# Splitting the second half's gated recurrence by time: eight steps ahead of the Runge-Kutta loop, twenty-four on GpSimd beside it

## The reference, cut to what matters

```
# x3: output of attention and MLP (B=32, T=32, D=256)
k    = x3 @ Wz.T + bz;   n = x3 @ Wn.T + bn
z    = sigmoid(k);       g(n) = n + 0.5 where n >= 0, else sigmoid(n)
h[t] = (1 - z[t]) * h[t-1] + z[t] * g(n[t]),   h[-1] = 0.5
x    = x + h                              # the "drive" of the ODE
q = p = cond
for t in range(32):                       # RK4, four derivative stages a step
    dq = q - q**3/3 - p + x[:, t] + tanh(q) @ coupling.T + bias
    dp = 0.08 * (q + 0.7 - 0.8 * p)
    q, p = rk4_step(...), clipped to +-20;   trace[:, t] = q
out = x + top4_blocks(gelu(trace @ W1.T)) @ W2.T
```

## Time and profile before

| | |
|---|---|
| median of three runs | 482.5 us |
| the profiled execution | 482.44 us |
| its span, first to last instruction | 480.6 us |
| TensorE busy | 467.4 us, 97% |
| VectorE busy | 389.3 us, 81% |
| ScalarE busy | 318.9 us, 66% |
| GpSimd busy | 48.0 us, 10% |

### The profile page before, as it was taken

One profiled execution on the slowest core, in us unless ns is written; L12 is line 12 of the kernel. 1 busy time (PEld: TensorE's weight loads), 2 busy tenths in 40 slices (PEclk: granted clock), 3 DMA queues, 4 the chain that ended last, 5 costly groups with the idle time before them and its releaser, 6 DMA issues.

```text
span 480.6 us, 13808 instructions
## 1 busy us (share of the span) xinstructions
PE 467.4 (97%) x5271; PEld 334.8 (70%) x5271; DVE 389.3 (81%) x1368; ACT 318.9 (66%) x950; POOL 48.0 (10%) x78
## 2 busy tenths in 40 slices
PE   7999999999999999999899999999999999999997
PEld 4455776557656676568545444788898988989886
DVE  4969895779768899997896997888888888888884
ACT  1677964788477966887476965565665656656563
POOL 3010240223020320223000000000000000000000
PEclk9999999999999999999999999999999999999999
DMA  8992510100201000000000000000000000000000
GB/s 283 419 388 70 135 45 22 62 25 23 66 22 44 22 0 2 0 2 1 1 1 1 0 1 0 3 3 1 0 1 11 12 0 12 0 12 11 1 12 23
DMA packets 10399, 20.85 MB, mean 43 GB/s; under 512 B 1472, under 2 KB 4992, under 8 KB 9728
## 3 DMA queue, kind: packets, MB, share of 16 engines
q1 hardware_dynamic: 9808, 19.89, 12.0%
q10 hardware_dynamic: 560, 0.60, 0.4%
HBM read 19.40 MB, written 1.08 MB: 43 GB/s over the span
## 4 chain that ended last, share of the span: by engine, by line
PE 88%; DVE 4%; ACT 3%; DMA 1%; issue 1%; POOL 1%; SPq 0%; DVEq 0%
PE bank L884 58%; PE score L884 27%; PE spare L884 2%; DMA ao_sb<-xtok 1%; POOL ptx L507 1%; ACT ptx L632 1%; ACT ao_sb L585 1%; DVE drive L1459 1%; ACT x L532 0%; ACT th L810 0%; DVE drive L1463 0%; DVE q_group L2112 0%; DVE tok_stats L1406 0%; DVE acc L1551 0%; DVE drive L1614 0%
## 5 line engine op out<-in xcount | busy, mean ns | idle before, releaser
L884 PE MATMUL bank<-x,pairs_store 128*128 128x512 f16 x384 | 86.3, 379 | 0.5 <-ACT x L532 0.4
L884 PEld LDWEIGHTS bank<-x,pairs_store 128*128 128x128 f16 x384 | 36.9, 98 | 43.4 <-issue 1.4
L507 POOL TENSOR_TENSOR ptx<-pt,ptx 32x256 f16<-32x256 f32 x62 | 43.2, 697 | 176.2 <-ACT ptx L632 172.8
L884 PE MATMUL score<-cub,neg_eye 128*128 128x64 f32 x256 | 55.6, 299 | 0.0
L585 ACT ACTIVATE big<-bank,head_b 128x512 f16<-128x512 f32 x60 | 39.8, 685 | 17.4 <-PE bank L884 17.0
L2026 DVE TENSOR_TENSOR thlo<-th 128x64 f16<-128x64 f32 x128 | 28.8, 225 | 26.0 <-ACT th L811 24.8
L884 PE MATMUL score<-th,coup_part 128*128 128x32 f16 x1024 | 46.2, 177 | 0.9
L884 PE MATMUL bank<-pairs_store,ao_sb 128*128 128x256 f16 x360 | 43.0, 273 | 0.7 <-issue 0.2
L884 PE MATMUL bank<-pairs_store,x 128*128 128x512 f16 x192 | 43.4, 379 | 0.0
L810 ACT ACTIVATE th<-score 128x64 f16<-128x64 f32 x96 | 21.5, 224 | 31.7 <-PE score L884 28.9
L884 PEld LDWEIGHTS bank<-pairs_store,ao_sb 128*128 128x128 f16 x360 | 34.0, 98 | 7.5 <-DVE ao_sb L1652 1.5
(11 more groups left out here) (252 smaller groups left out, 1052.1 us busy)
## 6 DMA issues: line engine op xcount, KB each, us to landing
wqk_sb<-wqk SPq DMA_DIRECT2D x16, 256.0 KB, 2.7
wv_sb<-wv SPq DMA_DIRECT2D x4, 512.0 KB, 5.4
wo_sb<-wo SPq DMA_DIRECT2D x4, 512.0 KB, 4.2
f_sb<-ffn_w SPq DMA_DIRECT2D x2, 1024.0 KB, 14.7
ao_sb<-xtok SPq DMA_DIRECT2D x4, 256.0 KB, 5.8
x_sb<-xT SPq DMA_DIRECT2D x1, 1024.0 KB, 12.5
w_sb<-w1T SPq DMA_DIRECT2D x1, 1024.0 KB, 16.1
w_sb<-w2T SPq DMA_DIRECT2D x1, 1024.0 KB, 16.9
```

Source lines behind the costliest of these rows:

```text
L507: nc.gpsimd.tensor_tensor(ptx[s, 1, :, s], pt[s], ptx[s, 0, :, s], ALU.subtract).then_inc(ptx_ready, 1)
L884: return nc.tensor.matmul(dst, lhsT, rhs, start=start, stop=stop, **kw)
```

## The change

The second half's columns are split by time instead of by batch. EARLY is steps 0 to 7 (16 batches x 8 = 128 columns a block, NE), LATE is steps 8 to 31 (384 columns a block, NL). TensorE multiplies EARLY of both blocks first. ScalarE makes three passes for a piece, all from PSUM: Tanh of z, Tanh of n, and Relu of n (the identity g = min(tanh, 0) + 1 + 2 relu, up to scale, replaces the first Relu). VectorE does EARLY of both blocks (`early_gru`), whose scan's last column is handed on.

LATE goes to GpSimd (`late_terms`): three tensor_scalar and two tensor_tensor passes of 384 columns, and the handed-on state folded into step 8 by two passes of 16 columns. VectorE scans LATE in eight pieces of 96 columns, at slot 1 of stages 6 to 13 of the loop's first round, in place of the eight low parts. GpSimd then adds x and splits the drive (`late_pair`): four passes of 384 columns a block, two of them written by time. A wait for both blocks' splits stands on VectorE at the second round's stage 15.

On ScalarE, `late_gates(0)` lies ahead of the EARLY drive's high parts, and `late_gates(1)`, three passes of 384 columns, after the first state's tanh, ahead of the loop. On TensorE the three matmuls that summed block 1's terms go, and 18 unread matmuls become 4.

```diff
-        za_last = centred[:, 0]
-        unit_row = pn[:].rearrange("p g t -> p (g t)").bitcast(F16)
+        EARLY, LATE = slice(0, 2 * UNROLL), slice(2 * UNROLL, T)
+        NBH = B // NH
+        NE, NL = NBH * 2 * UNROLL, NBH * (T - 2 * UNROLL)
+        parts_at = 2 * MB * P
+        early_store = big[:, parts_at:parts_at + KB * 6 * NE].rearrange("p (k w n) -> p k w n", k=KB, w=6)
+        parts_at += KB * 6 * NE
+        late_store = big[:, parts_at:parts_at + KB * 4 * NL].rearrange("p (k w n) -> p k w n", k=KB, w=4)
+        carry = sc[:, 0:KB, 0:NBH]
+        half_bn = tok_tmp[:, 0:KB]
...
-            nc.gpsimd.memset(unit_row, 1.0 / CSCALE).then_inc(unit_ready, 1)
+            def steps_of(ob):
+                return late_store[:, ob].rearrange("p w (b t) -> p w b t", b=NBH)
+            def later_steps(ap, ob):
+                return ap[:, ob, HALF:N].rearrange("p (b t) -> p b t", t=T)[:, :, LATE]
+            def late_terms(ob):
+                z, cand, pos, keep = (late_store[:, ob, w] for w in range(4))
+                use = USE_GRU[1] + ob
+                pool.wait_ge(free[bank_of(use)], count_of(use) + 1)
+                own.step(nc.gpsimd.tensor_scalar(keep, z, -0.5, 0.5, ALU.mult, ALU.add))
+                own.wait()
+                own.step(nc.gpsimd.tensor_scalar(z, z, 1.0, 0.25, ALU.add, ALU.mult))
+                pool.wait_ge(late_tanh, ob + 1)
+                own.step(nc.gpsimd.tensor_scalar(cand, cand, 0.0, 1.0, ALU.min, ALU.add))
+                use = USE_GRU[1] + 3 - ob
+                pool.wait_ge(free[bank_of(use)], count_of(use) + 1)
+                own.wait()
+                own.step(nc.gpsimd.tensor_tensor(cand, cand, pos, ALU.add))
+                own.wait()
+                own.step(nc.gpsimd.tensor_tensor(cand, cand, z, ALU.mult))
+                pool.wait_ge(z_used, KB + ob + 1)
+                _, cand, _, keep = (steps_of(ob)[:, w, :, 0] for w in range(4))
+                state = early_store[:, ob, 5].rearrange("p (b t) -> p b t", b=NBH)[:, :, 2 * UNROLL - 1]
+                own.step(nc.gpsimd.tensor_tensor(carry[:, ob], keep, state, ALU.mult))
+                own.wait()
+                own.step(nc.gpsimd.tensor_tensor(cand, cand, carry[:, ob], ALU.add))
+                own.wait()
+                nc.gpsimd.memset(keep, 0.0).then_inc(late_ready, 1)
+            def late_pair(ob):
+                at = slice(ob * B + NBH, (ob + 1) * B)
+                high, low = (drive_pair[:, c, LATE, at].rearrange("p t b -> p b t") for c in range(2))
+                shifted_drive = steps_of(ob)[:, 0]
+                pool.wait_ge(late_scanned, 4 * (ob + 1))
+                own.step(nc.gpsimd.tensor_tensor(later_steps(drive, ob), steps_of(ob)[:, 2], later_steps(x_sb, ob), ALU.add))
+                own.wait()
+                own.step(nc.gpsimd.tensor_scalar(shifted_drive, later_steps(drive, ob), c2_shifted[:, ob:ob + 1], None, ALU.add))
+                own.step(nc.gpsimd.tensor_scalar(high, later_steps(drive, ob), c2_shifted[:, ob:ob + 1], None, ALU.add))
+                own.wait()
+                nc.gpsimd.tensor_tensor(low, shifted_drive, high, ALU.subtract).then_inc(late_split, 1)
+            for ob in range(KB):
+                late_terms(ob)
+            for ob in range(KB):
+                late_pair(ob)
...
-            use = USE_GRU[1]
...
-            drive_bias(2, 4)
+            def gate_values(ob, z_in, n_in, out, z_done, tanh_done, n_done):
+                nc.scalar.activation(out[:, 0], z_in, ACT.Tanh, bias=hb[:, ob:ob + 1], scale=0.5).then_inc(z_done, 1)
+                if n_done is not early_gate:
+                    wait_product(USE_GRU[1] + 3 - ob)
+                nc.scalar.activation(out[:, 1], n_in, ACT.Tanh, bias=half_bn[:, ob:ob + 1], scale=0.5).then_inc(tanh_done, 1)
+                nc.scalar.activation(out[:, 2], n_in, ACT.Relu, bias=bn_twice[:, ob:ob + 1], scale=2.0).then_inc(n_done, 1)
+            def early_gates(ob):
+                src = (spare, score[:, 0])[ob]
+                act.wait_ge(early_full, ob + 1)
+                gate_values(ob, src[:, NE:2 * NE], src[:, 0:NE], early_store[:, ob], early_gate, early_gate, early_gate)
+            def late_gates(ob, both=True):
+                z_use, n_use = USE_GRU[1] + ob, USE_GRU[1] + 3 - ob
+                wait_product(z_use)
+                gate_values(ob, bank[bank_of(z_use)][:, 0:NL], bank[bank_of(n_use)][:, 0:NL], late_store[:, ob],
+                            free[bank_of(z_use)], late_tanh, free[bank_of(n_use)])
+            early_gates(0)
+            early_gates(1)
+            late_gates(0)
+            drive_bias(2, 3, EARLY)
+            drive_bias(3, 4, EARLY)
...
-            drive_bias(3, 5, slice(0, UNROLL))
-            drive_bias(3, 5, slice(UNROLL, T))
+            late_gates(1)
...
+                x3_steps = x3.rearrange("p k (b t) -> p k b t", t=T)
+                early_dst = (spare, score[:, 0])
+                def early(ob, k):
+                    for w, weights in enumerate((wn_sb, wz_sb)):
+                        last = mm(early_dst[ob][:, w * NE:(w + 1) * NE], weights[:, k, ob * P:(ob + 1) * P],
+                                  x3_steps[:, k, NBH:B, EARLY], k == 0 and w == 0, k == KB - 1, skip_group_check=True)
+                    return last
+                def late(use, weights, ob, k):
+                    dst = fill(use) if k == 0 else bank[bank_of(use)]
+                    last = mm(dst[:, 0:NL], weights[:, k, ob * P:(ob + 1) * P], x3_steps[:, k, NBH:B, LATE], k == 0, k == KB - 1)
+                    if k == KB - 1:
+                        last.then_inc(full[bank_of(use)], 1)
+                use = USE_GRU[1]
                 pe.wait_ge(x3_ready, KB + 1)
+                for ob in range(KB):
+                    early(ob, 0)
+                late(use, wz_sb, 0, 0)
                 pe.wait_ge(x3_ready, 2 * KB)
+                for ob in range(KB):
+                    early(ob, 1).then_inc(early_full, 1)
+                late(use, wz_sb, 0, 1)
+                for k in range(KB):
+                    late(use + 3, wn_sb, 0, k)
+                pe.wait_ge(early_gate, 3 * KB)
+                unread(score[:, 0], 1)
+                mm(score[:, 1], scaled_eye[:], ptx[:, 0, 0:G // 2].rearrange("p g n -> p (g n)"), True, True).then_inc(seeded, 1)
+                for k in range(KB):
+                    late(use + 1, wz_sb, 1, k)
+                for k in range(KB):
+                    late(use + 2, wn_sb, 1, k)
...
-            use = USE_GRU[1] + 2
...
-            unread(bank[bank_of(USE_GRU[1] + 1)][:], 18)
+            for use in (USE_GRU[1], USE_GRU[1] + 3):
+                pe.wait_ge(free[bank_of(use)], count_of(use) + 1)
+            unread(bank[bank_of(USE_GRU[1])][:], 4)
...
+            def early_gru(ob):
+                z, cand, pos, quarter, keep, state = (early_store[:, ob, w] for w in range(6))
+                dve.wait_ge(early_gate, 3 * ob + 1)
+                own.step(V.tensor_scalar(quarter, z, 1.0, 0.25, ALU.add, ALU.mult))
+                own.step(V.tensor_scalar(keep, z, -0.5, 0.5, ALU.mult, ALU.add))
+                dve.wait_ge(early_gate, 3 * ob + 3)
+                own.step(V.scalar_tensor_tensor(pos, cand, 0.0, pos, ALU.min, ALU.add))
+                own.wait()
+                own.step(V.scalar_tensor_tensor(cand, pos, 1.0, quarter, ALU.add, ALU.mult))
+                own.wait()
+                keep0, cand0 = (ap.rearrange("p (b t) -> p b t", b=NBH)[:, :, 0:1] for ap in (keep, cand))
+                own.step(V.scalar_tensor_tensor(cand0, keep0, 0.5, cand0, ALU.mult, ALU.add))
+                own.wait()
+                own.step(V.memset(keep0, 0.0))
+                own.wait()
+                own.step(V.tensor_tensor_scan(state, keep, cand, 0.0, ALU.mult, ALU.add))
+                own.wait()
+                early_steps = (ap[:, ob, HALF:N].rearrange("p (b t) -> p b t", t=T)[:, :, EARLY] for ap in (drive, x_sb))
+                early_drive, early_x = early_steps
+                V.tensor_tensor(early_drive, state.rearrange("p (b t) -> p b t", b=NBH), early_x, ALU.add).then_inc(z_used, 1)
+            def late_scan(piece):
+                ob, part = piece // 4, piece % 4
+                cols = slice(part * NL // 4, (part + 1) * NL // 4)
+                if part == 0:
+                    dve.wait_ge(late_ready, ob + 1)
+                V.tensor_tensor_scan(late_store[:, ob, 2, cols], late_store[:, ob, 3, cols], late_store[:, ob, 1, cols], 0.0,
+                                     ALU.mult, ALU.add).then_inc(late_scanned, 1)
...
-            use = USE_GRU[1]
...
-            drive_lows(2, 3, slice(0, UNROLL))
+            for m in range(MB):
+                V.memset(tok_shift[:, m:m + 1], 0.0).then_inc(h_low_ready, 1)
+            for ob in range(KB):
+                early_gru(ob)
+            drive_lows(2, 3, EARLY)
             dve.wait_ge(seeded, 1)
```

(34 more changed lines are left out.)

84 lines of the change are left out of this document (12 added, 72 removed).

## The result

The changed kernel is **slower by 0.5%**: 485.18 us (median of four executions, 484.7 to 486.15) against 482.68 for the kernel before, ratio 1.0054 with the interval 1.0041 to 1.0067. The forecast was 482.3 with a range of 478.6 to 484.6. All four executions have a mean granted clock of 0.986 to 0.993. The profiled one of before has 0.999, and the 70 executions of the kernel before that ran beside the experiments have 0.999 or 1.00.

The account below looks back on a forecast made before the run. Ahead of the loop, TensorE and ScalarE feed VectorE's recurrence; in the loop each stage is one closed circle. From 482.44, -4.4 + 2.8 + 0.9 + 0.7 - 0.1 = -0.1 gave 482.3 us, range 478.6 to 484.6.

Parts of the forecast that it names:

- The change with nothing in its way: Ahead of the loop, without GpSimd's holds: the second tanh comes at 301.3 instead of 305.67, a gain of 4.4 us.
- Hold ahead of the loop: Ahead of the loop, VectorE meets GpSimd's five late_terms(0) passes one by one: +2.8 us, bounds 0 and 3.9.
- Rival B: In late_terms and late_pair, GpSimd's one-input passes cost what two-input ones do, 0.94 at 384 columns: 484.9 us, chance 0.26.
- Stages 0 to 2: In the loop's first stages, one and a half late_terms(1) passes fall on VectorE's operations: +0.9 us, 0 to 1.5.
- late_pair twice: Over two to three stages a block, GpSimd's four passes delay thlo, the scans and first-stage operations: +0.7 us for both.
- TensorE idles: Ahead of the loop, TensorE waits 2.5 us because the low part is late; priced at 0.
- what would prove it wrong altogether: In round 0 a stage waits for late_ready, or TensorE's clock falls while it idles; no size given.
- GpSimd late: In the first two rounds, GpSimd's results come 6, 6 and 20 us ahead of need: 0.
- Rival C: Ahead of the loop, ScalarE, not the recurrence, sets the mark: under 0.5 us, inside every case; no chance of its own.
- Rival A: Ahead of and in the loop, the port lock bites less, 1.9 us of holds remaining: 479.8 us, chance 0.36.
- the slots: In VectorE's loop slots, eight scans of 2.9 us replace low parts of 3.6 us: -0.1 us.

Follow-up runs that it names:

- Experiment 5: The changed kernel with GpSimd's five late_terms passes a block replaced by memsets, leaving out the gates of steps 8 to 31; 481.22 us, ratio 0.9972.
- experiment 10: The changed kernel with smaller GpSimd pieces waiting on VectorE's stage signals, all late_terms inside the loop, later scans, late low parts on VectorE; 480.43 us, ratio 0.996.
- experiment 1: The changed kernel with 12 unread matmuls ahead of the loop instead of 4, filling TensorE's pause; 484.07 us, ratio 1.0037.
- experiment 2: The kernel before with 7 unread matmuls ahead of the loop instead of 18, so that TensorE pauses there; 484.42 us, ratio 1.0054.
- experiment 11: The kernel of experiment 10 with GpSimd's waits on VectorE's stage signals taken out, except the first; 481.49 us, ratio 0.9976.
- experiment 3: The kernel of experiment 1 with each block's four late_pair passes replaced by two GpSimd memsets of the float16 drive parts; 483.68 us, ratio 1.0029.

## Why the prediction was wrong

**The change with nothing in its way: right.** Forecast: low part 6.63 us behind x3 and mark 8.43 (299.5 and 301.3 less 292.87), gain 4.4. Experiment 5, nearly unheld: 6.61, 8.31, gain 4.5; experiment 10, where GpSimd has not begun: 6.47, 8.17, gain 4.6.

**Hold ahead of the loop, +2.8: mechanism right, size too large.** 1.8 at the mark (9.96 less experiment 10's 8.17), 2.1 at the last low part (8.57 less 6.47). VectorE met all five passes: 0.26, 0.31, 0.33, 0.66 and 0.74 over the plain lengths, against 0.4 + 0.5 + 0.5 + 0.6 + 0.8. The fifth (L2039 at 300.49, beside L546) reaches the last low part with 0.55, since that one starts at 301.70 where its high part was ready at 301.12. Of the 2.1 the mark gets 1.8: without holds ScalarE sets the mark, as the forecast had it, and from the last low part to the mark there are 1.70 in experiment 10, 1.39 here. Rival B was nearer in the durations (1.50 and 1.25 for two of the tensor_scalars) but not in the cost: L2007 met the pass of 1.50 and was let go 0.36 us behind its start.

**Stages 0 to 2, +0.9: right.** Behind the mark, stages 1 to 3 took 1.56 + 1.73 + 1.76 against 4.02 before (experiment 1, full clock): 1.03. In stage 0 one line (L2224) was held too, 0.56 for 0.23; that lies in the 1.8 above.

**late_pair twice, +0.7 (bounds 0.3 and 1.9): mis-sized.** 2.5 us, from experiment 1: stages 10, 11, 14 and 15 of the first round and 2 of the second took 0.56, 0.20, 0.65, 0.20 and 0.89 more than before. I halved the chance of meeting `thlo` because a waiting pass would start right behind it; the rows show GpSimd's two-input passes open when `thlo` comes (317.19, 329.13), 0.6 and 0.9 of delay each, and scans held in the slot just ahead of the next `thlo` too. Passes that write float16 at a step had no row near them, and L568 holds for 1.31 us, where I took 0.81.

**TensorE idles, "No row has a price; I take 0": the step that failed.** The pause was forecast (2.5 us; it was 2.0) and priced at nothing. In the kernel before such a pause costs 2.1 us when the clock falls to a mean of 0.993 (experiment 2). In the changed kernel's profiled execution, also at 0.993, it costs 1.08: stages 1 to 4 take 7.23 for experiment 1's 6.15 at full clock. The price is lower because these stages were held at the same time and the two delays overlap. By medians the changed kernel is 2.50 above its before, and experiment 1 at full clock 0.70 above its own; the 1.8 between them is the clock in all four executions, with what the loads at the start added (0.66 in the profiled one, not recorded for the others). At full clock the time would lie near 483.0, inside the range; this term carried it out. The last paragraph of the prediction names the fall of the clock as what would prove it wrong altogether; the range should have held a bound for it. The Trainium skill has the rule ("TensorE: Matmul & The Clock Gate", Part 1): how busy TensorE was of late sets whether it is granted the full clock. The trace agrees: the granted clock is 0.51 behind the pause, though one execution of five in experiment 2 kept 1.00. I had read that passage and gave it no chance of its own.

**GpSimd late: 0, right**; no stage waited for late_ready. **Rival C: out**: ScalarE's passes of 384 columns waited 0.25 us once for TensorE, and the mark without holds came at 8.17 for the forecast 8.43. **Rival A** is out too: VectorE was held by each of the five passes, and the holds sum to 5.2 us for A's 1.9.

At full clock experiment 1's lengths give -4.48 + 1.68 ahead of the mark, then +1.03 + 2.50 - 0.12 (the slots) and -0.05 behind stage 33: +0.56, and its executions at full clock measure +0.7. That the holds came out close is luck: 1.1 too much ahead of the mark and 1.8 too little in late_pair partly cancelled (4.4 forecast, 5.2 found). The clock had nothing to cancel it. One slip in the range: half way between 479.8 and 477.9 is 478.9, not 478.6; nothing hangs on it.

## What to carry to other kernels

A step that ends earlier on one engine can leave TensorE idle: give the pause a price of its own, and fill it with unread work or shorten it; look at the clock behind held stages too. Work handed to GpSimd beside VectorE costs by the passes that stand open when VectorE's critical operation comes, so keep its two-input passes short and start each one behind that operation; here shorter pieces, the later start, VectorE's signals and two passes less a block together turned +0.5% into -0.4%. The signals alone are worth 0.2 us in the stage times (experiment 11). Take the recorded length of a GpSimd pass for its time in its own chain, not for the hold.

## What the runs showed of the hardware

- GpSimd's one-input passes of 384 columns differ widely in length: 0.51 to 0.58 for multiply and add, 1.50 with a min, 1.25 with an addend per partition, 2.67 for that into float16 at a step of 128 bytes. But VectorE's two-input operations came free 0.35 to 0.44 us behind the start of each (L536, L538, L540, L565, L566 in the changed kernel), and `thlo` at 321.14 ran in 0.23 in the middle of the pass of 2.66.
- Two-input passes held until 0.13 to 0.15 us ahead of their recorded end, as the rows of before gave it, but L568, with its stepped float16 output, only until 0.65 ahead (twice).
- VectorE's tensor_scalar was held otherwise than its two-input operations: `ps<-pacc` (L2273) at 326.11 came free 0.14 us ahead of the end of the 1.25 us pass (L565), as it did at the memset of experiment 3. The same line at 320.25, inside the pass of 2.66, was not held (0.16); why is open.
- Memsets of 384 float16 columns at that step took 1.84 and 2.15, against 0.42 for 384 consecutive float32 ones.
- The same pause ahead of the loop lowered the clock in four executions of five (experiment 2) and not in the fifth. No run here tells which it will be.
